# Routing of the last two batches moved forward, and no POOL drain at four block ends, in a fused MoE-attention-MoE layer

## The reference

```python
x = x + 0.5 * ffn(layernorm(x), wg, shared_w1, shared_w2, expert_w1, expert_w2)
x = x + attn(layernorm(x), w_qkv, w_fproj, b_fproj, w_out, b_out)   # 16 heads of 64, rotary and Fourier terms
x = x + 0.5 * ffn(layernorm(x), ...)

def ffn(x):                       # all 2048 tokens flattened
    shared_out = swiglu(x, shared_w1, shared_w2)            # hidden 384
    gates = softmax(x @ wg.T)                               # 64 experts
    w_topk, idx_topk = top_k(gates, 8); w_topk /= w_topk.sum()
    # every (token, choice) gets a rank within its expert; ranks from 160 (CAPACITY) on are dropped
    h = einsum("ech,efh->ecf", buf, expert_w1); x1, x2 = split(h)
    out = einsum("ecf,ehf->ech", x1 * silu(x2), expert_w2)
    return shared_out + sum over the 8 choices of out[expert, rank] * weight
```

## Time and profile before

| what | value |
|---|---|
| median of 3 runs | 949.34 us (948.68 to 952.33) |
| the profiled execution | 948.54 us |
| its span | 946.8 us |
| mean granted TensorE clock | 0.969 of full |
| PE busy | 852.4 us (90%) |
| DVE, ACT, POOL busy | 574.8, 503.2, 486.4 us |
| longest wait of PE in the dense block | 5.27 us, for the rows of the first group |

### The profile page before, as it was taken

The page is one execution under the profiler, slowest core; times in us unless marked ns, Lnnn a source line. Parts: engine busy times, 40 slices in busy tenths (PEclk is TensorE's granted clock), DMA queues, the critical chain, the costliest instruction groups (busy, mean ns, idle before and its releaser), DMA issues. The chain is left out here.

```text
span 946.8 us, 19722 instructions
## 1 busy us (share of the span) xinstructions
PE 852.4 (90%) x6348; PEld 749.8 (79%) x6348; DVE 574.8 (61%) x1751; ACT 503.2 (53%) x1376; POOL 486.4 (51%) x517
## 2 busy tenths in 40 slices
PE   4689989999951899999999999999987999999968
PEld 3689989999950677777777777777687999999954
DVE  8946753333315777888888888877542367433437
ACT  3433333333310587888888888888841233333327
POOL 4036877777740322236666666666637444444450
PEclk9999999999985799999999999999998999999999
DMA  9826877787516690000000000000050397888738
GB/s 332 338 90 191 264 233 226 226 250 226 177 34 233 209 194 17 1 8 25 24 25 24 26 24 24 24 19 13 7 203 16 101 345 274 264 281 292 249 122 318
DMA packets 67938, 140.75 MB, mean 149 GB/s; under 512 B 10447, under 2 KB 37520, under 8 KB 67748
## 3 DMA queue, kind: packets, MB, share of 16 engines
q1 hardware_dynamic: 55232, 117.27, 38.0%
q0 software_dynamic: 11776, 21.39, 7.3%
q10 hardware_dynamic: 868, 1.31, 0.4%
HBM read 107.72 MB, written 35.56 MB: 151 GB/s over the span
## 5 line engine op out<-in xcount | busy, mean ns | idle before, releaser
L1752 POOL TENSOR_TENSOR at_m<-at_m 128x512 f32<-128x512 f32 x64 | 81.5, 1273 | 154.8 <-DVE at_m L1970 154.8
L1080 POOL DMA_INDIRECT xs_rows<-xr,slots_of x128 | 126.7, 990 | 42.1 <-issue 32.3
L2160 ACT ACTIVATE at_prob<-ps,at_nmax 128x256 f32<-128x256 f32 x256 | 117.8, 474 | 42.5 <-DVE at_nmax L1977 42.3
L1246 POOL DMA_INDIRECT y_rows<-f_og,f_put x80 | 80.1, 1001 | 97.6 <-ACT f_og L1400 78.1
L789 DVE TENSOR_TENSOR f_ehid<-f_esil,ps 128x480 f32<-128x480 f32 (+1 forms) x80 | 50.7, 634 | 121.4 <-ACT f_esil L667 113.5
L1538 DVE TENSOR_TENSOR f_hid<-f_sil,ps 128x480 f32<-128x480 f32 (+1 forms) x80 | 50.7, 634 | 115.9 <-ACT f_sil L1393 109.4
L1266 PE MATMUL ps<-f_xgT,f_ring 128*128 128x160 f32 x768 | 116.7, 302 | 1.7 <-issue 1.7
L524 POOL DMA_INDIRECT f_xg<-xn_rows,f_take x80 | 83.7, 1047 | 66.8 <-issue 66.8
L563 PE MATMUL ps<-f_xgT,f_ring 128*128 128x160 f32 x768 | 114.9, 299 | 0.2 <-issue 0.2
L1266 PEld LDWEIGHTS ps<-f_xgT,f_ring 128*128 128x128 f32 x768 | 108.6, 192 | 2.2 <-issue 2.2
L1393 ACT ACTIVATE f_sil<-ps 128x480 f32<-128x480 f32 (+1 forms) x80 | 44.3, 554 | 122.2 <-PE ps L1266 122.2
(11 more groups left out here) (253 smaller groups left out, 1843.3 us busy)
## 6 DMA issues: line engine op xcount, KB each, us to landing
f_ring<-in_wexp SPq DMA_DIRECT2D x128, 576.0 KB, 5.2
y_rows<-zeros SPq DMA_DIRECT2D x16, 512.0 KB, 5.9
at_yt<-y_rows SPq DMA_DIRECT2D x8, 1024.0 KB, 4.8
f_yt<-y_rows SPq DMA_DIRECT2D x16, 512.0 KB, 9.0
xs_rows<-at_blank SPq DMA_DIRECT2D x16, 342.5 KB, 9.8
f_xg<-xs_rows SPq DMA_DIRECT2D x16, 342.5 KB, 3.3
y_rows<-f_og,f_put POOLq DMA_INDIRECT x160
xs_rows<-xr,slots_of POOLq DMA_INDIRECT x128, 2.3
```

Source lines behind the costliest of these rows:

```text
L1080: nc.gpsimd.indirect_dma_start(xs_dram, bass.IndirectOffsetOnAxis(s.slots_of[:, t, k:k + 1], 0), s.xr[:, t, :], None, bounds_check=last_sl ...
L1246: nc.gpsimd.indirect_dma_start(ydram, bass.IndirectOffsetOnAxis(put[:, n:n + 1], 0), og[:, g, c, :], None, bounds_check=last_row, oob_is_e ...
L1752: nc.gpsimd.tensor_tensor(m1[:, p % 2, :], m1[:, p % 2, :], m2[:, p % 2, :], ALU.add).then_inc(msum, 1)
L2160: mm = nc.scalar.activation(prob[:, p % 2, h, t, :], ps[:, SB + h, t * SEQ:(t + 1) * SEQ], ACT.Exp, bias=nmax[:, p % 2, h, t:t + 1], accum ...
```

## The change

It has four parts. (a) The first four blocks get `no_gpsimd_drain=True`; the fifth does not. (b) Batch 6's ranks, places and list and its first four dispatches (choices 0 and 1) move from the dense block to the tail of attention. (c) The other dispatches are reordered: batch 6 choices 2 to 5 before the wait for batch 7's list, then batch 7 choices 0 to 3, batch 6 choices 6 and 7, batch 7 choices 4 to 7. `first_sent` and `rest_sent` are made in `build` and given to both blocks; what SP waits for is the same. (d) Batch 7's steps move two units forward: turn behind up(1) (was up(3)), logits at unit 1 (was 3), exp at 2 (was 4), ranks at 3 (was 5), list at 4 (was 6); the normalise moves ahead of the first product of DVE.

```diff
-            with nc.Block() as block:
+            with nc.Block(no_gpsimd_drain=True) as block:
...
@@ experts_dense, POOL
                 pick_root(nc, pool, s, BATCH - 1)
-                for half, sem in ((0, first_sent), (1, rest_sent)):
-                    for d in (BATCH - 2, BATCH - 1):
-                        pool.wait_ge(s.listed, 2 * d + 2)
-                        for k in choices(half):
-                            dispatch(nc, s, xs_dram, d, k, last_slot, sem)
+                for k in range(2, 6):
+                    dispatch(nc, s, xs_dram, BATCH - 2, k, last_slot, first_sent if k < HALF else rest_sent)
+                pool.wait_ge(s.listed, 2 * BATCH)
+                for k in choices(0):
+                    dispatch(nc, s, xs_dram, BATCH - 1, k, last_slot, first_sent)
+                for k in range(6, TOPK):
+                    dispatch(nc, s, xs_dram, BATCH - 2, k, last_slot, rest_sent)
+                for k in choices(1):
+                    dispatch(nc, s, xs_dram, BATCH - 1, k, last_slot, rest_sent)
@@ experts_dense, PE
-                pick_ranks(nc, pe, s, ranked, BATCH - 2)
                 shared_up(0, 0)
...
-                    if U == 2:
-                        pe.wait_ge(s.room_r, 3 * BATCH - 3)
+                    if U == 0:
                         pick_turn(nc, pe, s, turned, BATCH - 1)
+                    if U == 1:
+                        pick_logits(nc, pe, s, logit, BATCH - 1)
                     if U == 3:
-                        pick_logits(nc, pe, s, logit, BATCH - 1)
-                    if U == 5:
                         pe.wait_ge(s.room_r, 3 * BATCH - 1)
                         pick_ranks(nc, pe, s, ranked, BATCH - 1)
@@ experts_dense, DVE
                 pick_stats(nc, v, s, x, BATCH - 1)
+                pick_normalise(nc, v, s, x, BATCH - 1)
                 product(0, 0, SW)
-                pick_places(nc, v, s6, BATCH - 2)
...
-                    if U == 0:
-                        pick_list(nc, v, s, BATCH - 2)
                     if U == 1:
-                        pick_normalise(nc, v, s, x, BATCH - 1)
+                        pick_less_max(nc, v, s, BATCH - 1)
+                    if U == 2:
+                        pick_choose(nc, v, s7, BATCH - 1)
                     if U == 3:
-                        pick_less_max(nc, v, s, BATCH - 1)
+                        pick_places(nc, v, s7, BATCH - 1)
                     if U == 4:
-                        pick_choose(nc, v, s7, BATCH - 1)
-                    if U == 5:
-                        pick_places(nc, v, s7, BATCH - 1)
-                    if U == 6:
                         pick_list(nc, v, s, BATCH - 1)
@@ attention, POOL, behind the last keep_gates
+                        pool.wait_ge(s.listed, 2 * b)
+                        for k in range(2):
+                            dispatch(nc, s, xs_dram, b - 1, k, last_slot, first_sent)
@@ attention, PE, behind the last turn_p
+                pe.wait_ge(rope, PAIRS * BATCH)
+                pick_ranks(nc, pe, s, ps[:, QB, :], BATCH - 2)
@@ attention, DVE, ahead of residual
+                pick_places(nc, v, s6, BATCH - 2)
+                pick_list(nc, v, s, BATCH - 2)
@@ attention, ACT, behind the last take_p
+                pick_take_ranks(nc, act, s, ps[:, QB, :], BATCH - 2)
```

More of the change, by code:

```diff
@@ L1082, in dispatch, with experts_dense @@
             bounds_check=last_slot, oob_is_err=False).then_inc(sem, 16)
-def experts_dense(nc, x, wk, s, expert_key, slot_no, choice1, w, ydram, xs_dram, sent_in, ps, out_dram):
+def experts_dense(nc, x, wk, s, expert_key, slot_no, choice1, w, ydram, xs_dram, sents, ps, out_dram):
     wexp = w
@@ L1107, in experts_dense @@
         ident, shsb, xnT = s.ident, s.shsb, s.xnT
+        sent_in, first_sent, rest_sent = sents
         ring = esb("ring", [P, STEP_EXPERTS, WCOLS])
@@ L1133, in experts_dense @@
         sent = [esem(f"sent{g}") for g in range(SG)]
-        first_sent, rest_sent = esem("first_sent"), esem("rest_sent")
         xg_t, xg_s = esem("xg_t"), esem("xg_s")
@@ L1144, in experts_dense @@
         turned, logit, ranked = ps[:, GB, 0:256], ps[:, GB, 256:384], ps[:, GB, 384:512]
-        s6 = replace(s, place_now=s.place[:, TILES - 2 * TPB:TILES - TPB, :])
         s7 = replace(s, gate_now=s.gate[:, TILES - TPB:, :], top_now=s.top[:, TILES - TPB:, :],
@@ L1416, in step @@
                                 group_out(i, g, e - GE + 2)
-                pick_take_ranks(nc, act, s, ranked, BATCH - 2)
                 silu(0, 0, SW)
@@ L1430, in _ @@
                         silu(OPENING, 0, HW)
+                    if U == 0:
+                        pick_take_x(nc, act, s, turned, BATCH - 1)
+                        pick_row(nc, act, s, BATCH - 1)
+                    if U == 1:
+                        pick_take_logits(nc, act, s, logit, BATCH - 1)
                     if U == 2:
-                        pick_row(nc, act, s, BATCH - 1)
-                        pick_take_x(nc, act, s, turned, BATCH - 1)
+                        pick_exp(nc, act, s7, BATCH - 1)
                     if U == 3:
-                        pick_take_logits(nc, act, s, logit, BATCH - 1)
-                    if U == 4:
-                        pick_exp(nc, act, s7, BATCH - 1)
-                    if U == 5:
                         pick_take_ranks(nc, act, s, ranked, BATCH - 1)
@@ L1631, in _, with attention @@
                 join(QS // 2 - 1)
-def attention(nc, x, wk, ydram, attn_w, s, ps, wg, tables, xs_dram, sent_in):
+def attention(nc, x, wk, ydram, attn_w, s, ps, wg, tables, xs_dram, sents):
     (wqh, wql), (wvh, wvl), wout, wf, bf, bo, tabs, four = attn_w
     ident, res = s.ident, s.res
+    sent_in, first_sent, _ = sents
+    s6 = replace(s, place_now=s.place[:, TILES - 2 * TPB:TILES - TPB, :])
     slot_no, choice1, expert_key = tables
@@ L2258, in sem @@
             return ctx.enter_context(nc.semaphore(f"pick_{name}"))
-        sent_in = sem("sent_in")
+        sents = sem("sent_in"), sem("first_sent"), sem("rest_sent")
         pick = Pick(
@@ L2329, in build @@
             attn_w = (qk_parts, v_parts, t["wout"], t["wf"], t["bf"], t["bo"], (t["cos"], t["sin"]), t["four"])
-            attention(nc, x, wk, y_dram, attn_w, pick, ps, t["wg"], (slot_no, choice1, expert_key), xs_dram, sent_in)
-        experts_dense(nc, x, wk, pick, expert_key, slot_no, choice1, t["wexp"], y_dram, xs_dram, sent_in, ps, out)
+            attention(nc, x, wk, y_dram, attn_w, pick, ps, t["wg"], (slot_no, choice1, expert_key), xs_dram, sents)
+        experts_dense(nc, x, wk, pick, expert_key, slot_no, choice1, t["wexp"], y_dram, xs_dram, sents, ps, out)
 def tables():
```

1 line of the change is left out of this document (removed).

## The result

The changed kernel takes 936.81 us (median of 4 runs, 934.05 to 937.18) against 949.18 us before (4 runs, 948.68 to 952.33): ratio 0.9857, 95% interval 0.9828 to 0.9885. The forecast was 937.0 (934.5 to 942.5). The profiled execution took 936.77 us with a span of 935.0 us.

The account below looks back on a forecast made before the run. The chain to the first group's gather was taken to bound the second expert stage's start, with POOL's drain in the gap into attention. Terms -5.0 - 4.0 - 2.8 - 0.7 = -12.5 gave 937 us, range 934.5 to 942.5.

Parts of the forecast that it names:

- Term 1: Into attention: without POOL's drain the restart comes at 281.1 in place of 286.17, -5.0 us (bounds 0 and -5.2).
- second rival: Into attention: the gap isn't the drain's, so nothing is gained there, the rest as forecast: -7.5, 942 us; chance 0.09.
- The tail: Attention's end: four short products added on PE delay DVE's residual to 688.3, +0.2 us; batch 6's list is ready before.
- first rival: Attention's end: the barrier is held until POOL has made its four transfers, release at 693.2: -9.4, 940 us; chance 0.13.
- fourth rival: Attention's end: barrier waits for POOL's transfers under way, drain or not; release 701.9, +2.9, 952 us; slower from 699.0; chance 0.04.
- Term 2: Dense block's start: the chain from release to the first group's gather ends earlier, -4.0 us (bounds -2.4 and -5.3).
- Term 3: First group's products: with a wait of about 1 us PE's clock stays up, -2.8 us (bounds 0 and -2.96).
- term 4: Second group's gather: its last transfer goes 9.4 us earlier, so PE's 0.67 us wait vanishes, -0.7 us (bounds 0 and -0.7).
- third rival: Dense block's start: PE's hole of 2.8 to 3.7 us before the turn brings half clock: -11.9 to -11.0, 938 us; chance 0.72.

Follow-up runs that it names:

- e1: The kernel before with no_gpsimd_drain=True at the first four blocks and nothing else: 940.18 us, ratio 0.9916.
- e2: The changed kernel with the drain back at the end of the first expert block alone: 941.79 us, ratio 0.9926.
- e3: The changed kernel with the drain back at the end of attention alone: 947.17 us, ratio 1.0001.
- e4: The kernel before with batch 7's steps two units earlier on PE, ACT and DVE, drains and POOL's order as before: 946.99 us, ratio 0.9993.
- e8: The kernel of e4 with the drains gone at four block ends, without batch 6's move and POOL's new order: 940.66 us, ratio 0.9914.
- e9: The changed kernel with POOL's old dispatch order in the dense block, four dispatches still sent ahead: 942.52 us, ratio 0.9930.
- e5: The changed kernel again, unaltered, as comparison on the chip of the next three runs: 937.26 us, ratio 0.9872.
- e6: The changed kernel with only choice 0 of batch 6 (two dispatches) sent at attention's tail, choices 1 to 5 behind batch 7's root: 933.86 us, ratio 0.9843.
- e7: The changed kernel with batch 6's list still made at attention's tail but none of its dispatches sent there: 933.82 us, ratio 0.9837.

## Why the prediction was right

**Term 1 (-5.0).** -4.99 by the table, and e1 and e2 show that it is what the flag takes away: the gap closes with the flag alone (6.72 to 1.73 us) and opens again (6.72) when the flag is left out at this one block's end. That this is a drain is said by the flag's name alone; no view has a row for it. The second rival is refuted.

**The tail (+0.2).** The ranks' products on PE, five of them and not the four that I counted, lie at 678.68 to 678.99, before the last two `values`, and DVE's list is ready in time. The attention stage as a whole wasn't longer. The list was done 0.3 us ahead of the residual's start, so POOL's four dispatches began 0.3 us sooner than I had them.

**The first rival (barrier held by the four dispatches)** is refuted by one row: PE starts at 684.78 with dispatches at 683.88 to 688.7 under way.

**The fourth rival** had the right price for a drained block and the wrong condition. With the drain kept, e3, the restart comes 8.9 us behind POOL's last dispatch, as it had 8.7; without the drain, 0.4 us behind the residual. Its limit of 699.0 is where the sum would be zero; slower by the prediction's own 4.7 us would have been a release at 703.7 or later.

**Term 2 (-4.0).** The order of causes was as forecast: release, four dispatches, root, normalise, turn, list, eight dispatches, gather. The turn was 4.8 us nearer to the residual than before (forecast 4.4 with the tail's 0.2), the first dispatch of batch 7 4.2 and PE's start on the gathered rows 4.7. PE's wait for them was 1.00 us, as forecast. Right as a whole, 0.5 us small, and in one step by luck. The forecast kept the distance from batch 7's eighth dispatch to the rows, 6.71 us before (720.95 to 727.66); it came out at 6.17 (713.05 to 719.22), but its parts changed. Before, a 16 KB packet of instructions at 722.51 fell on the eighth dispatch's landing, and SP issued the gather 3.61 us behind that dispatch; now it is 2.18. Now such a packet (715.94) falls on the gather, which takes 3.99 us where it took 3.10. The forecast knew of neither.

**Term 3 and 4 (-2.8 and -0.7).** Together -3.59. Before, half clock stood behind the wait of 5.27 us (PEclk 0.50, PE busy 5.92 us), and half of that is the 2.96 of the forecast; now it is 1.00 in 719:725 behind 1.00 us. What the prediction did not price is how term 4 depends on the other parts: I had it as 0.7 us to gain, and it is a cost of some 5 us which the new order avoids (e4, e8 and e9), with batch 6's list made at the tail.

**The third rival (half clock behind the new hole)** happened in two of four traces of kernels with that hole (e2, e5) and not in the changed kernel's own or e9's. It costs 1.0 us in all, within the 0.6 to 1.5 that the rival's sum allows, but by another way: I had PE as the bound at the first group, and in e5 PE still waits there (0.85 us) and it is the chain that comes 1.2 us later. That PE starts slow behind this wait thus came in some executions only: 2.50 us of waiting (2.51 in e9) had both outcomes, PEclk 1.00 with a turn of 0.44 us, and 0.51 or 0.52 with a turn of 0.69 or 0.66.

**What cancelled.** The changed kernel's trace lost 1.6 us before attention, which no part of the change touches but for the flags, and gained 0.9 us more than forecast behind it. That the forecast time was met to 0.2 us is therefore in part luck. 0.5 of the 1.6 is there when the first expert stage begins, 0.9 in its first 24 products (the first row is before, the second after):

```profile
58.62 4.49 PE L563 MATMUL ps<-f_xnT,shsb 128*128 128x128 f32 x24 [4.10 <-PEq L154]
```

```profile
59.09 5.35 PE L563 MATMUL ps<-f_xnT,shsb 128*128 128x128 f32 x24 [4.17 <-PEq L154]
```

The same rows take 4.5 to 5.5 us in the eleven traces. I can't tell the flags from chance here. The three kernels with the drain at that stage's end have the three shortest (4.49, 4.56 in e2, 5.14 in e4; the others 5.35 to 5.46), and POOL's last L535 lies at 278.5 to 279.0 in them and at 279.6 to 280.3 in the eight without it. Yet the drain stands behind those products, and e2, which brings it back, costs 4.5 us or more where 5.0 less the 1.4 between e2's trace and the changed kernel's would be 3.6. Whether the flags cost up to 1.8 us there stays open.

## What to carry to other kernels

Before you move indirect transfers to the end of a block, look at how far POOL's last transfer lies from the restart there, and drop the drain first: here all but 2 us of its 8.74 was hidden while POOL stopped early, and with the move it showed, at 10.4 us by the medians (e3). In these kernels what reads the transfers' rows waits for their own semaphores, with the flag and without; no run tried it otherwise. When a chain that feeds several loads in turn is made earlier, work out the second load too; here making the first earlier alone gave nothing, because one engine issues for both. Put a short step that others wait for (here the root, 0.7 us) ahead of the queue of long ones: e6 and e7, which do, are 3.4 us better than the change as made.

## What the runs showed of the hardware

- A block's end with POOL's drain took long after indirect transfers: 8.7 and 8.9 us from the last dispatch's end to the restart (before, e3), 6.7 where the program also waits for them to land (before, e2). With the drain dropped the restart came 0.4 us behind the last work (684.37 to 684.78 in the changed kernel), and with the drain, where POOL had issued nothing for long, 0.3 (before).
- The same wait of PE ahead of the turn (2.50 us) left the granted clock at 1.00 in two traces (the changed kernel, e9) and was followed by 0.51 and 0.52 for 3.1 us in two others (e5, e2). Of the waits for a group's rows, those of 0.7 to 1.3 us (before, the changed kernel, e1, e2, e4 to e7, e9) never brought it down; those of 3.67 (e9), 3.82 (e4), 4.76 (e1), 4.92 (e8) and 5.27 us (before) each did, that of 3.67 only 1.5 us after PE had gone on.
- Twenty-four products of one shape took 2.92 us at a PEclk of 1.00 behind a wait of 0.94 us (685.04:688.10 in e1), and 4.39 (before), 5.47 (e4) and 5.46 us (e3) behind waits of 2.50, 2.50 and 13.77: the slow stretch had no fixed length. At 58.62 and 59.09 they took 4.49 and 5.35 us in spite of a PEclk of 1.00 in the windows there, so here the duration of the products told more than the window's figure.
- Where a packet of the instruction queue fell went with when data landed. Those of 16 KB that started from 711 to 723 us took 0.96 to 1.24 us. In the six traces in which one started 0.7 to 1.3 us behind the first group's issue (the changed kernel, e2, e4, e5, e6, e9), the rows came 3.8 to 4.3 us behind the issue; in the five in which none did (the kernel before, e1, e3, e7, e8), 2.9 to 3.1. In the kernel before and in e1 one fell on the landing of batch 7's eighth dispatch, and SP issued the gather 3.6 and 3.2 us behind that dispatch; in the other nine it was 2.1 to 2.2. In the slow gathers the last 0.7 to 1.1 us moved under 30 GB/s: 20 in 718.00:718.70 of the changed kernel and 19 in 715.40:716.10 of e6, where the ends of the quick ones had 257 (726.45:727.15 before) and 241 (716.05:716.75 in e7). This is a match in eleven traces; no run moved such a packet by itself, and why the end is slow no run shows.
